# A fifth addition on POOL per head, and one matmul group less on TensorE, in a fused attention layer

## The reference

```
h   = gamma * (layernorm(x) * ln_g + ln_b) + beta        gamma, beta from the condition vector
qkv = h @ Wqkv.T + bqkv                                   16 heads of 32 channels
att = softmax(q @ k.T, over the keys) / sqrt(512)
out = (att @ v) @ Wp.T + bp
h1  = out + x
y   = the same conditional layernorm of h1, plus h1
```

## Time and profile before

| | before |
|---|---|
| median of three runs | 1540.1 us |
| the profiled execution, its own time | 1545.36 us |
| its span in the profile | 1543.7 us |
| TensorE busy | 1388.2 us, 90% |
| POOL busy | 1030.1 us, 67% |
| DVE busy | 927.3 us, 60% |
| ACT busy | 718.3 us, 47% |
| granted TensorE clock, mean | 0.961 of 2.4 GHz |

### The profile page before, as it was taken

The page is one execution under the profiler, slowest core; times in us unless marked ns, Lnnn a source line. Parts: engine busy times, 40 slices in busy tenths (PEclk is TensorE's granted clock), DMA queues, the critical chain, the costliest instruction groups (busy, mean ns, idle before and its releaser), DMA issues.

```text
span 1543.7 us, 35342 instructions
## 1 busy us (share of the span) xinstructions
PE 1388.2 (90%) x10804; PEld 888.2 (58%) x10804; DVE 927.3 (60%) x1633; ACT 718.3 (47%) x1370; POOL 1030.1 (67%) x779
## 2 busy tenths in 40 slices
PE   6998999999999999999999999999898989899543
PEld 4887656565656566666666666666454545454233
DVE  5336666666666565666666666656566656565045
ACT  4221555555555454444555555455455555556200
POOL 2442556565655677677868777757777777778757
PEclk9999999999999999999999999999999999999766
DMA  6567443343434535342544535353323232322232
GB/s 221 167 187 201 114 99 110 84 123 82 121 85 123 133 103 144 106 135 71 164 106 130 136 103 144 83 153 90 105 75 105 78 103 78 105 75 57 63 110 82
DMA packets 219737, 175.62 MB, mean 114 GB/s; under 512 B 106740, under 2 KB 189684, under 8 KB 219672
## 3 DMA queue, kind: packets, MB, share of 16 engines
q1 hardware_dynamic: 217368, 167.46, 40.0%
q0 software_dynamic: 2304, 7.34, 1.2%
HBM read 114.87 MB, written 59.05 MB: 113 GB/s over the span
## 4 chain that ended last, share of the span: by engine, by line
PE 55%; POOL 15%; issue 13%; SPq 6%; DMA 4%; DVE 4%; POOLq 2%; ACT 1%; DVEq 0%; ACTq 0%
PE ps_a L660 11%; PE ps_o L691 9%; PE ps_st L674 9%; POOL p L1249 8%; PE ps_w L572 7%; PE ps_w L625 6%; PE ps_s L704 6%; PE ps_st L625 3%; SPq L423 2%; DMA q_stack<-max_rows 2%; POOL y_t L1227 1%; POOL y_t L1229 1%; POOL oT_s L1203 1%; DVE half_max L1048 1%; POOLq L1172 1%
## 5 line engine op out<-in xcount | busy, mean ns | idle before, releaser
L1048 DVE TENSOR_REDUCE half_max<-ps_a 128x1 f32<-128x512 f32 x1024 | 670.7, 687 | 420.6 <-PE ps_a L660 410.4
L1249 POOL TENSOR_TENSOR p<-p 128x1024 f32<-128x1024 f32 x256 | 610.8, 2388 | 341.7 <-PE ps_o L691 341.1
L858 ACT ACTIVATE p<-ps_st 128x512 f32<-128x512 f32 x1024 | 573.4, 597 | 507.2 <-PE ps_st L674 489.6
L660 PE MATMUL ps_a<-k_stack,q_stack 96*128 96x512 f32 x1024 | 455.5, 446 | 27.0 <-DVEq L1060 14.9
L674 PE MATMUL ps_st<-q_stack,k_stack 98*128 98x512 f32 x1024 | 417.6, 409 | 34.5 <-DMA q_stack<-max_rows 24.3
L660 PEld LDWEIGHTS ps_a<-k_stack,q_stack 96*128 96x128 f32 x1024 | 194.7, 190 | 216.3 <-issue 99.9
L691 PE MATMUL ps_o<-p,v_head 128*32 128x256 f32 x4096 | 274.6, 387 | 0.0
L674 PEld LDWEIGHTS ps_st<-q_stack,k_stack 98*128 98x128 f32 x1024 | 195.9, 192 | 74.6 <-issue 24.9
L691 PEld LDWEIGHTS ps_o<-p,v_head 128*32 128x32 f32 x4096 | 134.5, 111 | 99.2 <-issue 6.3
L704 PE MATMUL ps_s<-p,root_s 128*1 128x256 f32 x2048 | 160.3, 385 | 11.9 <-POOL p L1249 11.8
L625 PEld LDWEIGHTS ps_w<-hT_s,wqkv_s 128*128 128x128 f32 x1056 | 143.2, 190 | 10.8
(11 more groups left out here) (98 smaller groups left out, 971.3 us busy)
## 6 DMA issues: line engine op xcount, KB each, us to landing
qk_scratch<-qkT_s SPq DMA_DIRECT2D x108, 256.0 KB, 2.4
q_stack<-qk_scratch SPq DMA_DIRECT2D x192, 128.0 KB, 2.8
k_stack<-qk_scratch SPq DMA_DIRECT2D x192, 128.0 KB, 3.0
x_tile<-in_x SPq DMA_DIRECT2D x32, 256.0 KB, 5.0
gq_s<-gain_bias_scratch SPq DMA_DIRECT2D x16, 512.0 KB, 4.4
v_scratch<-v_parts SPq DMA_DIRECT2D x32, 256.0 KB, 3.2
v_head<-v_scratch SPq DMA_DIRECT2D x64, 128.0 KB, 2.1
att_scratch<-o_stage SPq DMA_DIRECT2D x256, 32.0 KB, 1.5
```

Of the source, the lines that this page charges most:

```text
L660: pe.matmul(ps_a[:, parity, :], q_stack[0:96, s, t * 128:(t + 1) * 128], k_stack[0:96, s, half * 512:(half + 1) * 512], start=True, stop=T ...
L858: nc.scalar.activation(p32[:, k, e * 512:(e + 1) * 512], ps_st[:, ST_BANK[2 * k + e], :], ACT.Exp).then_inc(exp_done, 1)
L1048: V.tensor_reduce(half_max[:, s % 2, item:item + 1], ps_a[:, parity, :], AX.X, ALU.max).then_inc(a_used, 1)
L1249: G.tensor_tensor(p32[:, 2 * j + 1, :], p32[:, 2 * j, :], p32[:, 2 * j + 1, :], ALU.add).then_inc(pair_added, 1)
```

## The change: five additions, three slabs

POOL gets a fifth addition per head, `half_add`: slot 1 (the sum of slots 0 and 1) is added to slot 3 (the sum of slots 2 and 3). TensorE multiplies three slabs (slots 3, 5 and 7) instead of four, in steps 1, 3 and 5 of the next head; the product in step 7 is gone. The waits follow: slot 1 is free for its next exponential when `half_add` is done; slots 3, 5 and 7 are freed by the three products. Four entries of the step tables are moved by one.

```diff
-NORM_SCALE_STEP = {7: 0, 11: 1}
+NORM_SCALE_STEP = {8: 0, 11: 1}
-RESIDUAL_STEP = {15: 0, 16: 1}
+RESIDUAL_STEP = {14: 0, 16: 1}
-OUT_LOW_STEP = {21: 0, 23: 1}
+OUT_LOW_STEP = {21: 0, 22: 1}
...
+        SUM_SLOT = [3, 5, 7]
+        SUM_READY = [3, 4, 5]
+        SLOT_FREE = {0: 1, 2: 2, 1: 3, 4: 4, 6: 5, 3: 1, 5: 2, 7: 3}
...
-                pe.wait_ge(pair_added, 16 * g + 4 * s + j + 1)
+                pe.wait_ge(pair_added, 20 * g + 5 * s + SUM_READY[j])
                 for e in range(4):
-                    mm = pe.matmul(ps_s[HD * e:HD * e + 1, 0:QW], root_s[:], p32[:, 2 * j + 1, e * QW:(e + 1) * QW],
-                                   start=(j == 0), stop=(j == 3))
+                    mm = pe.matmul(ps_s[HD * e:HD * e + 1, 0:QW], root_s[:], p32[:, SUM_SLOT[j], e * QW:(e + 1) * QW],
+                                   start=(j == 0), stop=(j == 2))
...
-                            if k == 7:
-                                pair_sums(i, s, 0)
-                            elif behind:
-                                pair_sums(*before, (k + 1) // 2)
+                            if k < 7 and behind:
+                                pair_sums(*before, k // 2)
...
-                freed = 16 * i + 4 * (step // 8) + k // 2 - 3
+                sums = k in SUM_SLOT
+                freed = (12 * i + 3 * (step // 8) - 3 if sums else 20 * i + 5 * (step // 8) - 5) + SLOT_FREE[k]
...
-                        need(act, sum_done if k % 2 else pair_added, freed)
+                        need(act, sum_done if sums else pair_added, freed)
...
+            def half_add(g, s):
+
+                pool.wait_ge(pair_added, 20 * g + 5 * s + 2)
+                G.tensor_tensor(p32[:, 3, :], p32[:, 1, :], p32[:, 3, :], ALU.add).then_inc(pair_added, 1)
...
+                    if k == 7:
+                        half_add(i, s)
```

More of the change, by code:

```diff
@@ L785, in _ @@
                 weighted(ITERS - 1, 3, k)
-            for j in range(1, 4):
+            for j in range(3):
                 pair_sums(ITERS - 1, 3, j)
@@ L844, in take_sums @@
             def take_sums(v, s):
-                act.wait_ge(sum_done, 4 * v + 4)
+                act.wait_ge(sum_done, 3 * v + 3)
                 nc.scalar.activation(o_stage[0:97, s % 2, QW:2 * QW], ps_s[0:97, 0:QW], ACT.Copy).then_inc(s_taken, 1)
```

## The result

The changed kernel takes 1569.48 us, the median of four runs (1563.86 to 1573.61). The kernel before takes 1542.58 us (1534.51 to 1549.79, four runs: the three behind the 1540.1 and one more). The ratio is 1.0173, 95% interval 1.0112 to 1.0235. The profiled execution has a span of 1568.2 us and a mean granted clock of 0.948, against 1543.7 us and 0.961 before, so 24.5 us are to be explained.

What follows compares the result with a forecast made beforehand. TensorE's issue bounds iterations with tiles, POOL's unbroken row the output-only boundaries. Terms -18.5 - 3.4 + 21.0 + 0.6 + 7.5 + 5 + 5.6 = +17.8 us on 1545.36; put on the 1540.1 median, 1558 us, range 1534 to 1574.

Steps and rivals of the forecast that it cites:

- The removed product: Each head's dropped slab product on TensorE: worth 0.43 us of issue; -18.5 us over heads 0 to 42, -3.4 over eight more.
- The fifth addition in ordinary heads: POOL's added 2.39 us addition away from boundaries: costs nothing, hidden by POOL's idle time, with 0.2 us to spare.
- The output-only boundary: Five boundaries into output-only iterations and the last: late POOL additions delay TensorE 4.2 us each, +21.0; clock +7.5 more.
- tile-and-output boundaries: Six boundaries into tile-and-output iterations: slot 1's exponential comes late, 0 to 1.7 us each, 0.8 taken, +5 us; no clock loss.
- The last iteration: POOL's unbroken row delays head 63's slot 1 exponential, +3.1 us, and the closing row, +2.4; together +5.6 us.
- The clock: TensorE at the lower 1.2 GHz level behind new output-only waits: 0 to 1.5 us each, upper end taken, 5 x 1.5 = +7.5.
- POOL's delay costs less: Rival, chance 0.34: clock stays up behind the new waits and tile-and-output boundaries hide theirs; +5.3 us, 1545 us, no change.
- TensorE stays the bound everywhere: Rival, chance 0.07: POOL finds 4.9 us of slack at a boundary, so the whole 27.5 us comes; 1513 us.
- POOL becomes the bound in tile-and-output iterations too: Rival, chance 0.12: ordinary heads miss the 0.2 us to spare, or every such boundary pays 1.7; 1566 to 1570 us.

Runs made afterwards that it cites:

- the kernel with the filled wait: Changed kernel plus twelve unread 512-column matmuls before the score matmul that waits at output-only boundaries, iterations 11 to 14; 1563.76 us, ratio 1.0095.
- the running sum: Changed kernel with its additions reordered, slot 1 into slot 2, then 2 into 3, so slot 1 comes free one addition earlier; 1552.84 us, ratio 1.0034.

## Why the prediction was right, step by step

The forecast was 1558 us, 1.2% slower, and the mechanism was POOL's row across boundaries. The result is 1.7% slower by the same mechanism, with one condition that the experiments add: how much of POOL's lateness reaches TensorE depends on the order in which the slots come free. Against the median of 1540.1 the forecast is a ratio of 1.0116, inside the measured interval, near its lower end. The terms against the profiled execution, in us:

```
                                            predicted   measured
start to the first exponential                  0         +2.3
tile-only iterations, removed product         - 6.9       -7.0
tile-and-output iterations: product           -11.6
                            boundaries        + 5.0
                            together          - 6.6       -5.3
output-only iterations: 4 x (4.2 + 1.5)
                        + 0.6 - 3.4           +20.0      +20.7
last iteration to the end: 5.7 + 5.6          +11.3      +13.8
sum                                           +17.8      +24.5
```

**The removed product** is worth 0.43 us a head: 7.0 us over 16 heads, 6.9 predicted, and -0.5% for the change in these iterations alone. Priced by busy time it would have been 10 us. Its busy time did fall by 37.7 us on the page; I had said that TensorE's as a whole would fall by some 30, and it fell by 7.6, since score and weighted matmuls that run at the lower clock are busy for longer (from the two pages, for the same numbers of records: weighted 281.9 us against 274.6, score 424.6 against 417.6).

**The fifth addition in ordinary heads** is free, as predicted: the tile-only stretch is the same with and without it (309.80 and 310.00). ACT waits for it in one head of each tile-only iteration, for 1.80 to 1.86 us, and TensorE's scores behind it don't wait.

**The output-only boundary.** Predicted were a wait of ACT of 4 to 5 us, 4.2 us at the score matmul and 1.5 us by the clock. ACT waited 3.65 us. The score matmul came at 1250.65 in place of 1248.08, in an iteration where ACT and POOL ran 1.1 us ahead of the kernel before (1222.02 against 1223.11): 3.7 us. The product of step 5, predicted at 1240.5 and so at 1239.4 with that 1.1 us, came at 1238.94. The 0.5 us by which both came sooner go back to a pause that I had overlooked in calling POOL's row unbroken. In the kernel before, POOL waits 0.74 us there for its own store to land; behind the first `half_add` the store landed sooner, and the same pause (at 1233.67) was 0.24 us:

```profile
1232.85 0.56 POOL L1173 TENSOR_TENSOR ostd_t<-ostd_t,minus_half 128x1 f32<-128x1 f32 x1 [0.74 <-issue]
```

From the score matmul's start to the start of the group behind the weighted matmuls TensorE took 3.39 us, and 1.84 in the kernel with the filled wait: 1.55 us for the clock, 1.5 predicted. The iterations are longer by 3.5, 5.4, 4.8 and 7.0 us in order, 5.2 in the mean for the 5.0 predicted. The spread isn't resolved. Two things in the 5.0 did not go as I said: TensorE does not wait at heads s = 2 to 3, where the sum has 0.15 us each, and the wait for the row maximum did change, from 3.26, 2.34, 2.62 and 2.74 us to 2.81, 1.85, 2.61 and 1.88. The closeness of 5.2 to 5.0 is in part luck.

**The mis-sized term: tile-and-output boundaries.** The prediction put them at 0.8 us each and their clock loss at nothing. Taken by itself the stretch missed by only 1.3 us, but that flatters the term. In the two iterations 5 and 6 the kernel before had stretches of lower clock in this profile (0.98 and 0.96 in the mean, 1.00 in the changed kernel); they are shorter by 3.7 and 2.5 us, more than the 1.7 that the products can give. In iterations 7 to 9 the change costs 0.5 to 0.9 us each where its products give 1.7: 2.2 to 2.6 us are lost, where 0.8 was predicted with 1.7 as the upper bound. Not all of that is the fifth addition. The kernel without it has two of these iterations at a clock of 1.00 as well, 7 and 9: they are 84.4 and 84.2 us long, 1.1 and 1.2 us less than before in place of 1.7. TensorE waits in each, 0.47 and 0.28 us, for an addition of DVE (`out_sum`, L1009) that it does not wait for in the kernel before. Against these two, the addition costs 1.6 and 2.1 us (85.95 and 86.24), about the upper bound. Over the seven iterations the stretch is 7.4 us shorter without it.

One thing that I had not counted is the pause in `power`: I read POOL's instructions and their idle times from 937.81 on the earlier trace rows, and not the pause of 1.91 us at 909.03 to 911.13 ahead of them. In the changed kernel it is 2.51, 2.59 and 3.01 us in iterations 7, 8 and 9, against 1.88, 2.06 and 1.91, as the stores land later there. Score matmuls then wait behind slot 1, here in two heads of an iteration:

```profile
920.53 0.50 PE L678 MATMUL ps_st<-q_stack,k_stack 98*128 98x512 f32 x1 [1.03 <-ACT p L861]
...
942.90 0.49 PE L678 MATMUL ps_st<-q_stack,k_stack 98*128 98x512 f32 x1 [0.56 <-ACT p L861]
```

With the store moved to SP, the loss of 2.2 to 2.6 us falls to 0.3 (the 1.4 us gained, of 1.7). Whether the longer pause or the whole row of work made it isn't told apart: the edit shortens both. But neither is enough without the wait for slot 1. In the kernel with added work that nobody waits for, POOL's row is longer still and the pauses are 2.0 to 3.3 us in iterations 5 to 9, and its iterations at a clock of 1.00 are within 0.4 us of before; and the running sum, with pauses of 2.2 to 2.8 us, has 85.0 us in iterations 7 to 9 in place of 86.1. In the changed kernel the clock did not fall behind its waits of 1.03 and 0.56 us: it is 1.00 in iterations 5 to 9.

**The last iteration** cost 13.8 us and not 11.3. From its start to the fourth head's score matmul (1430.77 before, the second of the row; 1450.65 after) the kernel fell back 9.2 us, where 5.7 + 3.1 = 8.8 was predicted. Behind it 4.6 us were lost instead of 2.5. The prediction had no clock loss there, though it had the same kind of wait (3.49 us) in its sum; the window behind it shows the lower level:

```profile
1450.60:1455.00 4.40, 4.35 (x27) 2.00 (x28) 0.00 (x0) 1.99 (x5) 2.39 (x2) 0.50 0.01 4
```

**The clock.** The choice of the upper end, 1.5 us per boundary, was right where the wait is (1.55 us at the one boundary that was compared; with matmuls in the wait it goes). Its effect on the whole time isn't shown. The Trainium skill, "TensorE: Matmul & The Clock Gate", section "HAM oscillation", says that waits for data let the clock fall back; the traces agree behind every wait of 2.58 us or more. Behind shorter ones they show both. The prediction had taken 1.28 us as a length that leaves the clock up, but in the same trace it fell behind a wait of 1.60 us, at 689.51, and stayed up behind one of 1.84, at 1033.01.

**The rivals.** "POOL's delay costs less" (1545) falls: the delay reached TensorE and the clock fell. "TensorE stays the bound everywhere" (1513) falls, and the kernel without the fifth addition took 23 us less, where the rival needs 27.5; its interval (17 to 28 us) doesn't exclude them. "POOL becomes the bound in tile-and-output iterations too" (1566 to 1570) was partly true. Its pay of 1.7 us or more was there in iterations 7 to 9, if what is missing from the products' gain is counted in; its condition for ordinary heads was not met. (Its 5 to 12 us on top of 1558 make 1563 to 1570, not 1566 to 1570.) The measured 1569.48 lies in its numbers, but mostly by another way: of the 6.7 us above my sum, 1.3 are in the tile-and-output stretch, 0.7 in the output-only one, 2.5 in the last iteration, and 2.3 at the start. That it still lies in my range of 1534 to 1574 is owed to the width of that range as well as to the mechanism.

**Left open.** The 2.3 us at the start: the first exponential comes after 153.4 to 153.9 us in the profiles of the three kernels that keep the old attention code, and after 154.5 to 156.3 us in those of the ten that hold the change in whole or in part, though no instruction of the change has run by then. No run looked for the cause. At the end of the first iteration the difference is 0.5 us (230.8 and 231.3 us), but that iteration has the change in it and is itself 1.8 us shorter, so the 2.3 us don't vanish: the gain of 7.0 us in the tile-only row comes on top of them.

## What to carry to other kernels

Price an instruction taken from the bounding engine by the distance of starts, and one given to an idle engine by its place in that engine's unbroken rows, not by its share of busy time: the same addition of 2.4 us was free in the tile-only heads and cost about 5 us at an output-only boundary, and so did added work whose result nobody waited for. Before moving work to an engine, list every pause in its queue with its cause. A pause that ends with a transfer changes when the work ahead of it moves (0.74 to 0.24 us at one boundary, 1.91 to 3.01 at another), and can be bought out: here that gave 0.6%, as much as the change in its best place (0.5%). Apply such a change where the idle time is, if the loops allow it, and order a sum so that the buffer that is wanted first comes free first.

## What the runs showed of the hardware

- POOL's drain did not end before POOL's own store had landed. At the six tile-and-output boundaries the pauses were 0.9 to 2.4 us before; after, they were 1.0 to 3.1 us at five and 0.24 us at the sixth, where the store had landed already. Where there is a pause, the instruction behind the drain starts some 0.2 us after the landing (911.13 behind 910.96, 903.47 behind 903.29). The stores ahead of the long pauses landed after 4.1 to 6.3 us. With the store on SP's queue the same drain took 0.14 us. A drain with another engine's transfer in flight was not tried apart.
- TensorE's granted clock fell to its lower level behind every wait of 2.58 us or more between the first and the last exponential of the 13 profiles. Behind waits of 1.2 to 2.5 us it did both: it fell behind 1.21 us (changed kernel, at 1148.06, 0.50 from 1148.80 to 1152.20) and stayed up behind 2.52 us (kernel before with SP's stores, at 1326.15, 1.00 from 1326.10 to 1330.10). It also fell with no wait over 0.5 us in the 5 us ahead (kernel before, 0.52 from 649.50 to 653.00). So the length of the last wait alone doesn't tell.
- Removing work from TensorE in front of a wait for a transfer bought little at the place that was compared: in iteration 11 the wait for `max_rows` ends 37.2 us behind the first exponential before, and 37.0 us in the kernel with three slabs and no fifth addition.
